# Attention scores from fp16 high and low parts, 96 rows per head, in place of block-diagonal fp32 keys

## What is computed

```python
x = x + conv_mix(group_norm(x))             # row and column state scans, gated mix
t = to_tokens(x)                            # 16 x 1024 x 192
t = t + attention(layer_norm(t))            # the part that changes
t = t + experts(layer_norm(t))              # 4 experts, top 2, 192 -> 768 -> 192

def attention(x):                           # 6 heads of 32 channels, L = 1024
    Q, K, V = (x @ W + b for W, b in ...)   # each split into 6 heads
    # token 0 attends to all keys; every other token to itself, the 16 keys to each side, and token 0
    s = Q . K * 32 ** -0.5                  # masked to the window
    return softmax(s) @ V @ Wo + bo
```

## Time and profile before

| | |
|---|---|
| median of 3 runs | 2994.44 us (2988.81 to 2997.75) |
| profiled execution: its own time | 2992.21 us |
| profiled execution: span of the trace | 2990.4 us |
| PE busy | 2495.5 us, 83% of the span |
| DVE busy | 1863.1 us, 62% |
| ACT busy | 1173.0 us, 39% |
| granted TensorE clock, mean | 0.92 |

### The profile page before, as it was taken

One profiled execution on the slowest core, in us unless ns is written; L12 is line 12 of the kernel. 1 busy time (PEld: TensorE's weight loads), 2 busy tenths in 40 slices (PEclk: granted clock), 3 DMA queues, 4 the chain that ended last, 5 costly groups with the idle time before them and its releaser, 6 DMA issues.

```text
span 2990.4 us, 50614 instructions
## 1 busy us (share of the span) xinstructions
PE 2495.5 (83%) x18147; PEld 1873.5 (63%) x18147; DVE 1863.1 (62%) x5249; ACT 1173.0 (39%) x3443; POOL 811.2 (27%) x656
## 2 busy tenths in 40 slices
PE   1349797889898998989898998999898989898397
PEld 0237575667676776767676766767676767666264
DVE  5346465666666666666666667666666766666254
ACT  0025343444343435344443435344444434353122
POOL 0000021323242312223232413133232324232344
PEclk9769797999999999999999999999999999999699
DMA  1540021324234242323332242333343331515464
GB/s 43 84 135 14 17 59 29 96 68 107 68 78 99 42 127 38 109 64 96 73 102 73 47 126 39 114 58 95 75 100 72 94 82 37 132 34 131 121 159 104
DMA packets 272442, 242.24 MB, mean 81 GB/s; under 512 B 208988, under 2 KB 250174, under 8 KB 261568
## 3 DMA queue, kind: packets, MB, share of 16 engines
q1 hardware_dynamic: 211456, 147.61, 18.3%
q0 software_dynamic: 50880, 52.59, 10.7%
q10 hardware_dynamic: 9856, 38.80, 4.0%
HBM read 133.73 MB, written 73.59 MB: 69 GB/s over the span
## 4 chain that ended last, share of the span: by engine, by line
PE 65%; DVE 20%; ACT 5%; issue 4%; DMA 1%; POOL 1%; SPq 1%; ACTq 0%; DVEq 0%; POOLq 0%
PE PSUM L1561 10%; PE PSUM L1609 7%; PE PSUM L1538 5%; PE PSUM L1631 5%; PE PSUM L1579 4%; PE PSUM L1581 3%; PE PSUM L1580 3%; DVE HLO L1084 3%; PE PSUM L1478 3%; PE PSUM L1434 2%; PE PSUM L1547 2%; DVE HHI L1081 2%; PE PSUM L1621 2%; PE PSUM L1475 2%; PE PSUM L1706 2%
## 5 line engine op out<-in xcount | busy, mean ns | idle before, releaser
L1561 PE MATMUL PSUM<-XT,WB 128*128 128x512 f16 x2010 | 529.2, 396 | 48.9 <-DMA META<-slots 43.5
L860 ACT ACTIVATE PSPT<-PSUM,NMX 94x126 f32<-94x126 f32 x1056 | 367.1, 358 | 368.3 <-PE PSUM L1621 188.7
L715 POOL DMA_INDIRECT out_dram<-Y,META x228 | 359.7, 1578 | 556.8 <-DVE Y L1108 437.1
L828 ACT ACTIVATE HF<-PSUM,WB 128x512 f32<-128x512 f32 x402 | 274.0, 686 | 530.1 <-PE PSUM L1561 529.0
L1579 PE MATMUL PSUM<-WB,HHI 128*128 128x192 f16 x1608 | 403.6, 251 | 46.6 <-DVE HLO L1084 45.3
L1580 PE MATMUL PSUM<-WB,HHI 128*128 128x192 f16 x1608 | 402.0, 250 | 0.0
L1581 PE MATMUL PSUM<-WB,HLO 128*128 128x192 f16 x1608 | 401.8, 250 | 0.0
L1081 DVE TENSOR_SCALAR HHI<-HF 128x512 f16<-128x512 f32 x402 | 178.0, 443 | 343.3 <-ACT HF L828 341.3
L1561 PEld LDWEIGHTS PSUM<-XT,WB 128*128 128x128 f16 x2010 | 198.8, 102 | 215.2 <-DMA META<-slots 43.6
L1609 PE MATMUL PSUM<-KBD,QT 128*94 128x378 f32 x704 | 304.5, 516 | 9.1 <-ACT PSPT L860 7.4
L1084 DVE SCALAR_TENSOR_TENSOR HLO<-HF,HHI 128x512 f16<-128x512 f32 x402 | 278.3, 692 | 13.8
(11 more groups left out here) (272 smaller groups left out, 4405.9 us busy)
## 6 DMA issues: line engine op xcount, KB each, us to landing
WB<-weights SPq DMA_DIRECT2D x67, 1600.0 KB, 6.8
XR<-in_x ACTq DMA_DIRECT2D x16, 768.0 KB, 5.2
out_dram<-X ACTq DMA_DIRECT2D x32, 384.0 KB, 3.0
weights<-WB ACTq DMA_DIRECT2D x4, 1600.0 KB, 6.5
GUP<-TGU SPq DMA_DIRECT2D x256, 8.0 KB, 1.8
slots<-XROW,IDX POOLq DMA_INDIRECT x256
out_dram<-Y,META POOLq DMA_INDIRECT x228, 3.6
HF<-in_w ACTq DMA_DIRECT2D x6, 384.0 KB, 4.7
```

What stands on the lines that cost most here:

```text
L715: pool.indirect_dma_start(out[:, :], bass.IndirectOffsetOnAxis(row, 0), Y[:, wslot(i, j), q, :], None, bounds_check=B * T + BS - 1, oob_is ...
L828: act.activation(HF[:, k % 2, :], PSUM[:, 4 + k % 2, :], ACT.Gelu, scale=1 / (X_UP * W_UP), bias=bias).then_inc(f["gelu_done"], 1)
L860: e = act.activation(PS[0:QS, n % 2, h, :], PSUM[0:QS, n % 2, h * KS:(h + 1) * KS], ACT.Exp, bias=NMX[:, b, n % 2, h:h + 1], accum_out=DEN ...
L1561: mm = pe.matmul(dst, WB[:, ws, w:w + 128], XT[:, xs, chunk, :], start=(n == 0), stop=(n == 4))
```

## The change

Queries and keys are each written as the sum of an fp16 number (high part) and the fp16 rest (low part). A product is then high x high + high x low + low x high. The three terms are laid under each other: QS3 holds, for every head on its own, 32 rows of high, 32 of high again and 32 of low queries; KS3 holds high, low and high keys in the same 96 rows. One fp16 multiplication over 96 rows thus gives the scores of one head.

- PE: the mask multiplication comes first in a score unit, then three fp16 multiplications of 126 columns, one for each head.
- ACT evacuates all 12 query and key pieces, twice each: `high_part` writes the fp16 high part and then the whole value in fp32 to WIDE, two slots in turn. It no longer takes value pieces.
- DVE makes the low parts (`low_part_of_piece`: WIDE minus high) and evacuates all six value pieces.
- SP spreads the parts over the partitions: `spread(i)` issues 36 DMAs for an image, nine for each of (q0, q1, k0, k1), each of 32 partitions with 2068 B (queries) or 2772 B (keys).
- PE waits for all four groups before the first score of an image. A projection piece waits for the evacuation of the piece four before it, as before.
- Small buffers (H1, H1T, TM, EM) share a tensor MIXED with WIDE; the key parts lie in XN and PSPT, the query parts in QT. Setup clears QS3 and KS3 in place of KBD.

```diff
-        KBD = sb("KBD", [128, 2, NB, HH, KS])
+        QTALL = QT[:].rearrange("p a b q -> p (a b q)")
+        QPARTS = QTALL.bitcast(F16).rearrange("p (s a b q) -> p s a b q", s=2, a=2, b=NB)
+        QS3 = sb("QS3", [128, HEADS, NB, QS], F16)
+        KS3 = sb("KS3", [128, HEADS, NB, KS], F16)
...
-                    for t in (XWF, KBD, XG, PSPT):
+                    for t in (XWF, QS3, KS3, XG, PSPT):
                         dve.memset(t[:], 0.0)
...
+        def high_part(act, n):
+
+            oh, b0, b1, width = widths(n)
+            src = bank(n % 4)[0:HC]
             if n < 6:
...
+                bias, scale = BQS[:, oh:oh + 1], UNSCALE * HD ** -0.5
+                parts = [(QPARTS[0:HC, 0, oh, b0:b1, 1:QS], src[:, 0:width].rearrange("p (b q) -> p b q", q=QB))]
                 if n % 3 == 2:
...
+                    parts.append((QPARTS[0:HC, 0, oh, :, 0], src[:, width:width + 1].broadcast_to((HC, NB))))
+                    width += 1
             else:
...
+                bias, scale = BK[:, oh:oh + 1], UNSCALE
+                parts = [(KHIGH[0:HC, oh, b0:b1, :], src[:, 0:width].rearrange("p (b q) -> p b q", q=KS))]
+            for dst, ps in parts:
+                act.activation(dst, ps, ACT.Identity, bias=bias, scale=scale)
+            act.activation(WIDE[0:HC, n % 2, 0:width], src[:, 0:width], ACT.Identity, bias=bias, scale=scale
+                           ).then_inc(s["piece_act"], 1)
+
+        def low_part_of_piece(dve, n):
...
+            for dst, high, whole in parts:
+                last = dve.scalar_tensor_tensor(dst, whole, 1.0, high, ALU.mult, ALU.subtract)
+            last.then_inc(s["qk_low"], 1)
...
+            def spread(i):
+
+                for kind, dst, parts in (("q", QS3, (QPARTS[:, 0], QPARTS[:, 0], QPARTS[:, 1])),
+                                         ("k", KS3, (KHIGH, KLOW, KHIGH))):
+                    for oh in range(2):
+                        sp.wait_ge(s["qk_low"], at("qk_low", i, (6 if kind == "k" else 0) + 3 * oh + 3))
+                        for h in range(HH):
+                            for r in range(3):
+                                sp.dma_start(dst[r * HD:(r + 1) * HD, oh * HH + h, :, :],
+                                             parts[r][h * HD:(h + 1) * HD, oh, :, :]
+                                             ).then_inc(s[f"{kind}{oh}_spread"], 16)
...
             moves_in(1)
+            spread(0)
             for i in range(B):
...
                 if has(i + 2):
                     moves_in(i + 2)
+                if has(i + 1):
+                    spread(i + 1)
...
-                for n in range(PIECES):
+                for n in range(12):
                     yield from slot.until(PIECE_SLOT + n)
-                    if n % 2 == 0:
-                        act.wait_ge(s["piece_done"], at("piece_done", i, n + 1))
-                        evacuate_piece(act, n, s["piece_act"])
+                    act.wait_ge(s["piece_done"], at("piece_done", i, n + 1))
+                    if n >= 2:
+                        act.wait_ge(s["qk_low"], at("qk_low", i, n - 1))
+                    high_part(act, n)
...
                 for n in range(PIECES):
                     yield from slot.until(PIECE_SLOT + n)
-                    if n % 2 == 1:
+                    if 1 <= n <= 12:
+                        dve.wait_ge(s["piece_act"], at("piece_act", i, n))
+                        low_part_of_piece(dve, n - 1)
+                    if n >= 12:
                         dve.wait_ge(s["piece_done"], at("piece_done", i, n + 1))
-                        evacuate_piece(dve, n, s["piece_dve"])
+                        evacuate_values(dve, n)
...
             def attention(i, stream):
                 before = not first(i)
                 side = (mix(i + 1),) if has(i + 1) else ()
-                pe.wait_ge(s["piece_act"], at("piece_act", i, PIECES // 2))
-                pe.wait_ge(s["piece_dve"], at("piece_dve", i, PIECES // 2))
+                pe.wait_ge(s["piece_act"], at("piece_act", i, 12))
+                pe.wait_ge(s["piece_dve"], at("piece_dve", i, 6))
+                for kind in ("q0", "k0", "q1", "k1"):
+                    pe.wait_ge(s[kind + "_spread"], at(kind + "_spread", i, 16 * 9))
 
                 def scores(n):
                     b, oh = n // 2, n % 2
                     if n >= 2:
                         pe.wait_ge(s["exp_done"], at("exp_done", i, n - 1))
-                    pe.matmul(PSUM[0:QS, n % 2, 0:HH * KS], QT[:, oh, b, :],
-                              KBD[:, oh, b, :, :].rearrange("p h k -> p (h k)"), start=True, stop=False)
                     v = 0 if b == 0 else 2 if b == NB - 1 else 1
-                    pe.matmul(PSUM[0:QS, n % 2, 0:HH * KS], EYEB[:], MASKB[:, v, :], start=False, stop=True
-                              ).then_inc(s["score_done"], 1)
+                    pe.matmul(PSUM[0:QS, n % 2, 0:HH * KS], EYEB[:], MASKB[:, v, :], start=True, stop=False,
+                              skip_group_check=True)
+                    for h in range(HH):
+                        mm = pe.matmul(PSUM[0:QS, n % 2, h * KS:(h + 1) * KS], QS3[:, oh * HH + h, b, :],
+                                       KS3[:, oh * HH + h, b, :], start=False, stop=(h == HH - 1),
+                                       skip_group_check=True)
+                    mm.then_inc(s["score_done"], 1)
```

More of the change, by code:

```diff
@@ L156, in hybrid_kernel @@
         RDEN = sb("RDEN", [QS, NB, 2, HH])
-        PSPT = sb("PSPT", [128, 2 * HH * (KS + QS)])
+        PSPT = sb("PSPT", [128, NB * KS])
+        KHIGH, KLOW = (t.bitcast(F16)[:, 0:2 * NB * KS].rearrange("p (a b k) -> p a b k", a=2, b=NB)
+                       for t in (XN[:].rearrange("p t c -> p (t c)"), PSPT[:]))
         PS = PSPT[:, 0:2 * HH * KS].rearrange("p (a h k) -> p a h k", a=2, h=HH)
-        PT = PSPT[0:KS, 2 * HH * KS:].rearrange("p (a h q) -> p a h q", a=2, h=HH)
+        PT = PSPT[0:KS, 2 * HH * KS:2 * HH * (KS + QS)].rearrange("p (a h q) -> p a h q", a=2, h=HH)
         XNT = PSPT[0:HC, 0:2 * NH].rearrange("p (j t) -> p j t", j=2)
         OS = XWF[:].rearrange("p (b c) -> p b c", b=NB)
-        OT = QT[:].rearrange("p a b q -> p (a b q)")[:, 0:2 * T].rearrange("p (a t) -> p a t", a=2)
+        OT = QTALL[:, 0:2 * T].rearrange("p (a t) -> p a t", a=2)
         CM = sb("CM", [1, HEADS])
@@ L518, in evacuate_piece @@
                 if n % 3 == 2:
-                    col = src[0:HC, 400:401].broadcast_to((HC, NB))
-                    parts.append((QT[0:HC, oh, :, 0], col))
-                for dst, ps in parts:
-                    if is_act:
-                        last = eng.activation(dst, ps, ACT.Identity, bias=BQS[:, oh:oh + 1], scale=UNSCALE * HD ** -0.5)
-                    else:
-                        last = eng.tensor_scalar(dst, ps, UNSCALE * HD ** -0.5, BQS[:, oh:oh + 1], ALU.mult, ALU.add)
-            elif n < 12:
-                oh, (b0, b1) = (n - 6) // 3, SPANS[n % 3]
-                k = b1 - b0
-                for h in range(HH):
-                    p = slice(h * HD, (h + 1) * HD)
-                    dst = KBD[p, oh, b0:b1, h, :]
-                    ps = src[p, 0:k * KS].rearrange("p (b q) -> p b q", b=k)
-                    if is_act:
-                        last = eng.activation(dst, ps, ACT.Identity, bias=BK[p, oh:oh + 1], scale=UNSCALE)
-                    else:
-                        last = eng.tensor_scalar(dst, ps, UNSCALE, BK[p, oh:oh + 1], ALU.mult, ALU.add)
-            else:
-                b0 = 2 * (n - 12)
-                k = min(2, NB - b0)
-                dst = VW[:, b0:b0 + k, :]
-                ps = src[0:KS, 0:k * C].rearrange("p (b q) -> p b q", b=k)
-                if is_act:
-                    last = eng.activation(dst, ps, ACT.Copy, scale=UNSCALE)
-                else:
-                    last = eng.tensor_scalar(dst, ps, UNSCALE, None, ALU.mult)
@@ L546, in evacuate_piece @@
-            last.then_inc(give, 1)
+                    parts.append((QPARTS[0:HC, 0, oh, :, 0], src[:, width:width + 1].broadcast_to((HC, NB))))
+                    width += 1
+            else:
+                bias, scale = BK[:, oh:oh + 1], UNSCALE
[4 more added lines that the diff above has]
+                           ).then_inc(s["piece_act"], 1)
@@ new lines, in low_part_of_piece @@
+        def low_part_of_piece(dve, n):
+            oh, b0, b1, width = widths(n)
+            wide = WIDE[0:HC, n % 2, :]
+            if n < 6:
+                parts = [(QPARTS[0:HC, 1, oh, b0:b1, 1:QS], QPARTS[0:HC, 0, oh, b0:b1, 1:QS],
+                          wide[:, 0:width].rearrange("p (b q) -> p b q", q=QB))]
+                if n % 3 == 2:
+                    parts.append((QPARTS[0:HC, 1, oh, :, 0], QPARTS[0:HC, 0, oh, :, 0],
+                                  wide[:, width:width + 1].broadcast_to((HC, NB))))
+            else:
+                parts = [(KLOW[0:HC, oh, b0:b1, :], KHIGH[0:HC, oh, b0:b1, :],
```

(11 more changed lines are left out.)

28 lines of the change are left out of this document (14 added, 14 removed).

## The result

The change made the kernel slower: 3181.69 us, median of 4 runs (3164.82 to 3196.36), against 2991.62 (2984.85 to 2997.75), a ratio of 1.063 (95% interval 1.058 to 1.068). The profiled execution took 3164.82 us, its span 3163.0, 172.6 more than the span before; the mean granted clock fell from 0.92 to 0.83. Of the runs further down, one execution of e7_before_fill (3004.07 us) was a slow one and is left out of its ratio.

The account below looks back on a forecast made before the run. TensorE was taken as the bound, with DVE in some attention iterations. Images 0 to 14 save 5.0 us each (75), image 15 4.5, images 0 and 1 lose 9: 70 less, median 2923 us, range 2868 to 2990.

Parts of the forecast that it names:

- Score unit: Score units on PE: three fp16 matmuls at 0.056 us replace the fp32 pair, 0.80 to 0.33 us a unit.
- What it shortens: Attention loop: thinner score units save 7.0 us per image with the clock as now, mostly where PE bounds.
- ACT and DVE: Projection stage: ACT's 4.5 to 4.8 us per chunk fits barely in PE's 5.2; DVE gets about 1 us more.
- lag and gain: Projection stage: 0.4 us per image charged for lag, 0.5 us won at its end by an earlier last gelu.
- DMA issue: 36 spread DMAs per image on SP at 0.42 us per issue, bounds 0.34 and 0.71; a group of nine 3.8 us.
- No queue forms: SP's spreads in images 2 to 15: groups become ready about 5 us apart, each issued in 3.8 us.
- Landing: Last spread DMA lands in 2.6 us, hidden with 1.4 us of cover; images 0 and 1 lose 9 us in all.
- the rival: Spread becomes the wait before scores in every image: 2 to 5 us exposed, 2951 to 2993 us; chance 0.16.
- The clock: Attention loop: the clock falls two iterations earlier, in 4 and 5 instead of 6, costing 2.1 us per image.
- the third rival: Low clock spreads over attention iterations 1 to 6 and the kernel is slower, 3051 us; chance 0.13.
- The clock without idle time: Attention iterations from 3 on: less PE work brings the fall earlier, 2.1 us per image, iteration 7 at full clock.
- The rest: Image 15, with no mix beside its attention, saves 4.5 us; clearing QS3 and KS3 in setup costs nothing, up to 5.

Follow-up runs that it names:

- e7_before_fill: Kernel before the change, with twenty multiplications that nothing reads ahead of the transposes of iteration 5; 2948.67 us, ratio 0.985.
- e12: Changed kernel with later XR load, merged query spreads, high parts spread first, ACT issuing some spreads in images 0 to 2, TensorE gaps filled; 2924.04 us, ratio 0.978.
- e2: Changed kernel without its 36 spreading DMAs per image and the waits for them, scores taken from zeros; 2968.55 us, ratio 0.992.
- e9: e2 with TensorE waiting ahead of each attention for four small DMAs issued one after another; 3231.49 us, ratio 1.079.

## Why the prediction was wrong

The sum was -70 us; the profiled execution gave +173. In the order of its steps:

- **Score unit**: right. 0.33 us, three matmuls as near to each other as forecast. The rule of the Trainium skill against which it was weighed (TensorE: Matmul & The Clock Gate, section Back-to-back issue gap) would have had 0.40, an estimate from its 81 ns; the trace does not agree with it.
- **What it shortens**: too high. With the clock held in both, e12 against e7, a loop is 49.5 against 55.3 us: 5.8 of the 7.0. Iterations 1 and 2 gave 1.0 each (0.8 and 0.6 said), but 0 only 0.3 where no spread delays it (it waits for DVE), 6 0.5 (0.94), and 7 to 9 0.5 each in place of 0.93 (TensorE now waits 0.3 us in each for a sum of the mix from DVE).
- **ACT and DVE**: right that they fit; lag and gain were both nil. First query piece to first score is 30.5 us before and 30.6 in e2. The last low part was ready 7.9 us ahead of TensorE's last work in front of the scores (7.8 said).
- **DMA issue**: the step that began it. I took 0.42 us near; it was 0.59, one every 0.63. "No queue forms" failed with it: a group is 5.7 us and groups come about 5 apart. The high bound of 0.71 held, and by it 1 to 5 us were exposed; I gave that case 0.16.
- **Landing**: 2.1 us by itself, 4.1 to 5.7 beside the XR load, which the rival had named. Both together are the rival's 2 to 5 us in images 3 to 13, and 14 us in images 0 to 2: there the whole train of 22.8 us is the pace, not ACT, and image 2 belongs to them. 92 us more in place of 9: 83 of the 243 us by which I missed.
- **The clock**: the largest failure. "A stretch at 1.2 GHz makes PE busy throughout, and after such a stretch the clock rises again" was my argument against the third rival, and it does not hold for thin units: e9 shows 24 us of unbroken busy time, iterations 0 to 2, without a rise, in all 15 images with a mix. I knew the fall of iteration 5 and never asked what 4 us of idle time would do. This is worth 84 us (loops of 953 against 869 in e2).
- **The clock without idle time**: place right (iterations 3 and 4), price wrong. 2.1 us an image were charged; a loop of e2 takes 7.1 us more than one of e12, one of the kernel before 1.7 more than one of e7 at full clock, so the change costs about 5 more than today. It lasts into iteration 7, which I had at full clock. With the shortening above it makes loops 23 us shorter in e2, where 78 were said: 55 us of the miss.
- **The rest**: the loop of image 15 gave 3.7 us (4.5 said), but nothing came of it: behind it TensorE waits for the tokens of the experts, 9.7 us in place of 4.7, and comes to its first expert multiplication 51.1 us after the first score, before 50.1. The stretches outside the loops took 19 us more; this wait is 5 of them, and a longer stay at half clock between the loops (28 us more) up to 14.

Two rivals came together, with one causing the other: the spread became the wait, and the wait set the clock. I had priced them as if they excluded each other (2951 to 2993, and 3051).

## What to carry to other kernels

Before making TensorE's units thinner, ask what it does after the next wait: thin work may hold full clock and still often fail to win it back. Price a train of DMAs by the gap between issues of its own kind, times their number, and look at what else is issued where it ends. Where an engine waits anyway, filling the gap ahead of a fall of the clock can be worth more than the work saved (44 us for twenty multiplications an image that nothing reads). Then read the stretch behind the one that was shortened: a transfer that was just hidden can be its new wait.
